# A mamba and mixture-of-experts layer on one core: the same steps in another order on every engine

## The reference

```python
h = layernorm(x) * (1 + ca) + sa
zxbcdt = h @ W_in                       # 256 -> 1288: z 512, xBC 768, dt 8
xBC = silu(causal_conv4(xBC) + conv_b)
dt = softplus(dt + dt_bias)             # cumulative sums of dt*A give the decays
y = ssd(x, dt, A, B, C) + x * D         # 8 heads of 64, 128 states
y = rmsnorm(y * silu(z)) * norm_w
x = x + ga * (y @ W_out)
h = layernorm(x) * (1 + cb) + sb
w = softmax(h @ gate_w + gate_b); w = normalise(where(w >= 0.1, w, 0))
x = x + gb * sum_e w[e] * (h @ expert_w[e] + expert_b[e])      # 8 experts, 256 x 256
```

## Time and profile before

| what | us |
|---|---|
| median of three runs | 2529.53 (2528.25 to 2530.95) |
| the profiled execution, its own time | 2541.7 |
| its span, first to last instruction | 2539.9 |
| PE busy | 2344.5 (92%) |
| DVE busy | 1958.5 (77%) |
| ACT busy | 1716.6 (68%) |
| POOL busy | 1618.7 (64%) |

### The profile page before, as it was taken

One profiled execution on the slowest core, in us unless ns is written; L12 is line 12 of the kernel. 1 busy time (PEld: TensorE's weight loads), 2 busy tenths in 40 slices (PEclk: granted clock), 3 DMA queues, 4 the chain that ended last, 5 costly groups with the idle time before them and its releaser, 6 DMA issues. The chain is left out here.

```text
span 2539.9 us, 48735 instructions
## 1 busy us (share of the span) xinstructions
PE 2344.5 (92%) x14936; PEld 1941.9 (76%) x14936; DVE 1958.5 (77%) x4070; ACT 1716.6 (68%) x4364; POOL 1618.7 (64%) x1812
## 2 busy tenths in 40 slices
PE   2689999999999999999999999999999999999998
PEld 2567787787778787778777777878777878777776
DVE  4378887887787887788788778788878878877863
ACT  1377776777777677776677777767777767777662
POOL 1145666766666676666676666667666667666676
PEclk6599999999999999999999999999999999999999
DMA  3000000000000000000000000000000000000000
GB/s 106 13 16 18 24 11 25 26 24 24 24 20 14 26 26 24 22 24 12 24 26 24 22 26 20 14 26 26 24 22 24 11 25 26 24 22 18 16 13 21
DMA packets 62927, 59.12 MB, mean 23 GB/s; under 512 B 10096, under 2 KB 62160, under 8 KB 62672
## 3 DMA queue, kind: packets, MB, share of 16 engines
q1 hardware_dynamic: 62672, 56.01, 7.2%
HBM read 39.22 MB, written 16.78 MB: 22 GB/s over the span
## 5 line engine op out<-in xcount | busy, mean ns | idle before, releaser
L858 DVE SCALAR_TENSOR_TENSOR feat<-pa,cw,feat 128x512 f32<-128x512 f32 x576 | 429.4, 745 | 73.4 <-ACT feat L547 65.2
L1163 PE MATMUL pe<-e_hi,h_hi 128*128 128x512 f32 x1024 | 448.6, 438 | 4.4 <-ACT eacc L682 2.3
L1163 PE MATMUL pe<-e_lo,h_hi 128*128 128x512 f32 x1024 | 413.1, 403 | 0.0
L1163 PE MATMUL pe<-e_hi,h_lo 128*128 128x512 f32 x1024 | 412.1, 402 | 0.0
L547 ACT ACTIVATE feat<-pa,cb,cw 128x512 f32<-128x512 f32 x192 | 149.3, 778 | 289.9 <-PE pa L1163 289.9
L1048 DVE SCALAR_TENSOR_TENSOR eacc<-pe,wg,eacc 128x256 f32<-128x256 f32 x512 | 245.3, 479 | 104.4 <-PE pe L1163 94.0
L620 ACT ACTIVATE lm<-lm,lndt 128x128 f32<-128x128 f32 x1024 | 325.1, 395 | 0.0
L609 ACT ACTIVATE lm<-pd,e3in 128x128 f32<-128x128 f32 x1024 | 278.8, 387 | 55.1 <-PE pd L1163 53.5
L401 POOL TENSOR_TENSOR rs<-ssq,neghalf 128x1 f32<-128x1 f32 x128 | 70.4, 550 | 356.7 <-ACT ysq L636 356.7
L1163 PE MATMUL pa<-h_hi,w_hi 128*128 128x260 f32 x768 | 244.5, 318 | 49.1 <-DVE feat L858 24.8
L692 ACT ACTIVATE ex<-pe,wg 128x256 f32<-128x256 f32 x512 | 212.9, 468 | 82.9 <-issue 43.8
(11 more groups left out here) (173 smaller groups left out, 6555.4 us busy)
## 6 DMA issues: line engine op xcount, KB each, us to landing
xin<-_attn_hidden_states_dram SPq DMA_DIRECT2D x32, 512.0 KB, 4.3
xres<-_attn_hidden_states_dram SPq DMA_DIRECT2D x128, 128.0 KB, 2.1
out_dram<-x SPq DMA_DIRECT2D x128, 128.0 KB, 2.2
feat<-in_L_wmod_dram SPq DMA_DIRECT2D x1, 1536.0 KB, 6.6
feat<-in_L_attn_W_in_dram SPq DMA_DIRECT2D x1, 1024.0 KB, 5.9
gz<-in_L_ffn_expert_w_dram SPq DMA_DIRECT2D x1, 1024.0 KB, 9.0
x<-in_L_ffn_expert_w_dram SPq DMA_DIRECT2D x1, 1024.0 KB, 11.3
mm<-in_L_attn_W_out_dram SPq DMA_DIRECT2D x1, 512.0 KB, 6.9
```

What stands on the lines that cost most here:

```text
L858: dve.scalar_tensor_tensor(out=acc, in0=pa[:, :, 1 + j:1 + j + HT], scalar=cw[:, f, j:j + 1], in1=acc, op0=ALU.mult, op1=ALU.add).then_inc ...
L1163: return pe.matmul(o, lhsT=l, rhs=r, start=start, stop=stop, skip_group_check=True)
```

## The change

Only the order in the five lists is new. Every step is issued as often as before, for the same tiles, with the same waits in it and on the same engine; no buffer changes. POOL's loop starts one pass earlier, so that `halo` can be written as `n + 4`. PE's list has the same 72 steps and DVE's the same 101; ACT's has 69, POOL's 55, SP's 9. The order differs in nearly every place. The piece of the diff around the cumulative sums, DVE first, then PE, then POOL:

```diff
             for n in range(-4, NTILE + 16, T):
...
                 do(dts_, dve, n - 4)
-                do(S_, dve, n - 6)
-                do(xD0, dve, n - 12)
-                do(xn2_, dve, n - 8)
+                do(xn2_, dve, n - 7)
+                do(x2_, dve, n - 6)
                 do(n_hi, dve, n)
                 do(cse_, dve, n - 4)
-                do(xn2_, dve, n - 7)
-                do(yTlo_, dve, n - 6)
-                do(gs_, dve, n - 5)
                 do(parts_, dve, n - 4)
+                do(M_, dve, n - 5)
+                do(st2_, dve, n - 6)
+                do(xD0, dve, n - 12)
+                do(es_, dve, n - 4)
+                do(lg_, dve, n - 8)
                 do(n_hi, dve, n + 2)
-                do(M_, dve, n - 5)
-                do(xD1, dve, n - 12)
-                do(y1_, dve, n - 5)
-                do(es_, dve, n - 4)
                 do(S_, dve, n - 5)
...
+                do(state_, pe, n - 5)
                 do(cs_, pe, n - 4)
-                do(xT_, pe, n - 5)
+                do(h2T_, pe, n - 8)
+                do(e3_, pe, n - 12)
                 do(hT_, pe, n + 2)
-                do(e2, pe, n - 12)
-                do(h2T_, pe, n - 8)
-                do(yoff_, pe, n - 5)
+                do(e0, pe, n - 12)
+                do(lgm_, pe, n - 8)
+                do(bias_, pe, n - 11)
                 do(csT_, pe, n - 4)
-                do(wout_, pe, n - 6)
-                do(ft0, pe, n)
-                do(bias_, pe, n - 11)
-                do(state_, pe, n - 5)
-                do(lgm_, pe, n - 8)
                 do(ydiag_, pe, n - 5)
                 do(D_, pe, n - 4)
+                do(xT_, pe, n - 4)
+                do(ft0, pe, n)
...
                 do(ve2_, pool, n - 8)
                 do(out_, pool, n - 14)
-                do(halo, pool, n)
-                do(y2_, pool, n - 6)
+                do(scd_, pool, n - 5)
+                do(xd_, pool, n - 5)
+                do(rs_, pool, n - 6)
+                do(rstd2_, pool, n - 8)
+                do(xs_, pool, n - 5)
                 do(exs_, pool, n - 13)
-                do(scd_, pool, n - 6)
-                do(rstd2_, pool, n - 8)
                 do(exb_, pool, n - 13)
                 do(n_lo, pool, n)
+                do(x2r_, pool, n - 6)
                 do(eall_, pool, n - 13)
-                do(h2lo_, pool, n - 10)
-                do(xs_, pool, n - 5)
                 do(og_, pool, n - 13)
+                do(exs_, pool, n - 12)
                 do(n_lo, pool, n + 2)
```

More of the change, by code:

```diff
@@ L448, in out_ @@
                 pool.tensor_tensor(x2[:, x.n % NX2], ex[:, x.j, 0], x2[:, x.n % NX2], ALU.add).then_inc(S["out"], 1)
-            for n in range(0, NTILE + 16, T):
+            for n in range(-4, NTILE + 16, T):
+                do(eall_, pool, n - 15)
+                do(exs_, pool, n - 14)
+                do(n_ve, pool, n)
+                do(exb_, pool, n - 14)
+                do(n_rstd, pool, n)
+                do(og_, pool, n - 15)
+                do(x2r_, pool, n - 8)
                 do(out_, pool, n - 15)
[L452 to L455, removed]
+                do(h2lo_, pool, n - 10)
+                do(xs_, pool, n - 6)
@@ L1077, in _ @@
+                do(xD1, dve, n - 15)
                 do(tA3, dve, n - 4)
-                do(ag2_, dve, n - 9)
-                do(xD0, dve, n - 14)
                 do(tB3, dve, n - 4)
                 do(tC3, dve, n - 4)
-                do(yTlo_, dve, n - 8)
-                do(y1_, dve, n - 7)
-                do(xn2_, dve, n - 10)
-                do(xn2_, dve, n - 9)
+                do(n_st, dve, n + 3)
+                do(x2_, dve, n - 8)
+                do(lg_, dve, n - 10)
+                do(M_, dve, n - 7)
@@ L1382, in _ @@
-                do(bias_, pe, n - 13)
-                do(h2T_, pe, n - 10)
-                do(wout_, pe, n - 8)
-                do(e1, pe, n - 13)
-                do(lgm_, pe, n - 10)
-                do(ft5, pe, n - 4)
-                do(e0, pe, n - 13)
+                do(wout_, pe, n - 8)
+                do(h2T_, pe, n - 10)
+                do(e3_, pe, n - 14)
+                do(lgm_, pe, n - 10)
+                do(ft4, pe, n - 4)
+                do(e0, pe, n - 14)
+                do(state_, pe, n - 7)
@@ L1403, in _ @@
-                do(bias_, pe, n - 12)
-                do(yoff_, pe, n - 6)
-                do(D_, pe, n - 5)
-                do(z_, pe, n - 1)
-                do(e1, pe, n - 12)
-                do(ydiag_, pe, n - 6)
-                do(state_, pe, n - 6)
-                do(hT_, pe, n)
-                do(e0, pe, n - 12)
-                do(e3_, pe, n - 12)
+                do(bias_, pe, n - 13)
+                do(ft5, pe, n - 4)
+                do(xT_, pe, n - 6)
+                do(e2, pe, n - 14)
@@ new lines, in _ @@
+                do(G_, pe, n - 6)
+                do(yT_, pe, n - 7)
+                do(e1, pe, n - 13)
+                do(yoff_, pe, n - 6)
+                do(wout_, pe, n - 7)
+                do(e0, pe, n - 13)
+                do(z_, pe, n - 4)
+                do(D_, pe, n - 5)
+                do(state_, pe, n - 6)
+                do(z_, pe, n - 3)
+                do(ydiag_, pe, n - 6)
+                do(z_, pe, n - 2)
+                do(xT_, pe, n - 5)
+                do(e3_, pe, n - 13)
@@ L1413, in _ @@
                 do(yT_, pe, n - 6)
                 do(G_, pe, n - 5)
+                do(z_, pe, n - 1)
+                do(gt_, pe, n - 12)
+                do(e2, pe, n - 13)
+                do(wgT_, pe, n - 12)
+                do(yoff_, pe, n - 5)
+                do(hT_, pe, n)
+                do(bias_, pe, n - 12)
+                do(wout_, pe, n - 6)
+                do(e1, pe, n - 12)
+                do(state_, pe, n - 5)
                 do(cs_, pe, n - 4)
-                do(xT_, pe, n - 5)
+                do(h2T_, pe, n - 8)
```

274 lines of the change are left out of this document (129 added, 145 removed).

## The result

The changed kernel takes 2378.77 us (2377.07 to 2385.10), the kernel before, timed beside it, 2530.24 us (2528.25 to 2532.53): a ratio of 0.9406, 95% interval 0.9386 to 0.9425. The profiled execution of the changed kernel took 2377.07 us, its span is 2375.3 us, against 2539.9 us before, so the two traces differ by 164.6 us.

What follows compares the result with a forecast made beforehand. PE's own work was taken as the bound: 70.9 + 0.2 + 1.15 + 0.5 + 0.15 = 72.9 us a group against 75.06, 58 us over 27 groups plus 1.9 at the end, giving 2470 us, range 2440 to 2532.

Steps and rivals of the forecast that it cites:

- PE's own work sets the pace and cannot shrink: Steady groups: PE's busy 70.9 us a group stays, as no instruction is removed; only idle and low-clock time can be won.
- wait between `csT_` and `ft0`: PE waits about 1.15 us a group there in small pieces, instead of 1.6 + 0.65 = 2.25.
- small waits shown (taps, `yT_`): PE waits 0.5 us a group for convolution taps and for `yT_` behind ACT's decays; bounds 0 and 1.3.
- low clock: Steady groups: PE's clock drops cost 0.15 us a group instead of 0.64; bounds 0 and 0.64.
- share of `gt_`: The extra `gt_` step in some groups adds 0.2 us to the average group.
- From `cs_` to `ft0`: Path through DVE and POOL takes 9.0 us beside 7.86 us of PE's own work.
- The low clock follows these two gaps: PE's clock falls after its standstills of 1.6 us before `csT_` and 0.65 us before `ft0`.
- Nothing: Start, to 383 us: bound by conv taps and loads that keep their durations, so no gain.
- At the end: Six expert steps instead of three cover PE's idle time ahead of the expert weights' transpose, so 1.9 us go.
- POOL's queue comes late: POOL's `ve2_` waits for DVE's later `ag2_`, delaying fifteen steps behind it; slower, about 2546 us at 5.3 us late; chance 0.13.
- Turns eat most of it: DVE and POOL block each other, PE waits 2.6 us at `ft0`; 2496 to 2524 us; chance 0.20.
- All of it: `parts_` meets less of POOL, the path fits into 7.86 us; 71.3 us a group, 2430 us; chance 0.11.

Runs made afterwards that it cites:

- light_after: Changed kernel with convolution taps, decays, `M_` and POOL's sums of y and experts' results cut to 8 columns, own order kept; 2348.64 us.
- light_before: Kernel before with convolution taps, decays, `M_` and POOL's sums of y and experts' results cut to 8 columns, old order kept; 2366.87 us.
- turns_after: Changed kernel with POOL's `h2lo_` moved back between the two `n_lo`, so one more POOL operation is ready beside `parts_`; 2417.17 us, ratio 0.9522 to the kernel before.
- cover_less: Changed kernel with one expert step, `e3_`, moved on PE from behind `cs_` and `h2T_` to ahead of `cs_`; 2435.97 us, ratio 0.9603 to the kernel before.
- lgm_before: Kernel before with `lgm_` moved on PE to directly behind `csT_`; 2521.59 us, ratio 0.9942.
- parts_first: Kernel before with `parts_` moved on DVE to right behind `cse_`, ahead of `xn2_`, `yTlo_` and `gs_`; 2588.64 us, ratio 1.0191.
- pe_cover: Kernel before with `ft0` moved two steps back on PE, behind `bias_` and `lgm_`; 2530.78 us, ratio 0.9984.
- light_lgm: light_before with `lgm_` moved on PE to directly behind `csT_`; 2353.66 us.
- light_g: light_lgm with one `G_` moved on PE from ahead of `gt_` and `xT_` to behind `xT_`; 2358.88 us.

## Why the prediction was right and wrong

The direction and the place were right. PE's idle time was the larger part of what an order could win, the largest piece of it stood at `csT_` and `ft0`, and turns between DVE and POOL made `parts_` late. The size was not. The 2.84 us a group between forecast and result come from two steps: the floor under PE's time (1.3), and the waits that I expected to stay (1.15 and 0.5).

**The step that failed: "PE's own work sets the pace and cannot shrink".** I took the busy 70.89 us of a group as a floor and could then win at most 3.3 us of idle time. The floor is no higher than 69.2 us, by `light_after`. For the old list `light_before` shows 1.0 us of waits inside the busy time, and by the estimate above, with the two waits for the state taken off, it is 1.5 us and 69.4 are left. A group lost 74.24 - 69.6 = 4.6 us undisturbed, more than all its idle time. With this floor even a forecast without any wait would have had 70.9 + 0.2 = 71.1 us a group, 107 us less, or about 2420, where 2379 was measured. The size of the other step, the waits that were to stay, is taken apart under the table.

**The sum against the measurement**, for a group, in us:

| term | forecast | measured |
|---|---|---|
| PE's own work, small hidden waits included | 70.9 | 69.6 |
| wait between `csT_` and `ft0` | 1.15 | 0 |
| small waits shown (taps, `yT_`) | 0.5 | 0 |
| low clock | 0.15 | 0.2 |
| share of `gt_` | 0.2 | 0.23 |
| sum | 72.9 | 70.06 |

The row on the clock is the mean of 70.06 less 69.6 and less the `gt_` share (six groups with about 1.03 us more). The 2.84 us between the sums make 77 us over 27 groups.

**From `cs_` to `ft0`.** The path was forecast at 9.0 us, 8.9 without the handover, and measured at 8.10 (775.81, the start of `cs_`, to 783.91). `parts_` has 1.95 instead of 2.98: I had counted how many operations POOL has ready there and not how long they are. `es_` has 0.5 instead of 0.9. `M_` has 1.68 instead of 1.13, which fits a wait for POOL's `og_` (778.49 to 779.27). The cover is 8.44 and not 7.86. So a wait of 1.15 became 0.24 to spare. `turns_after` shows that the 2.98 had not been a bad number for the case it was made for: with one more POOL operation in reach the four take 2.92. The path was treated as a sum of fixed prices; `cover_less`, with 0.9 us for the same four, shows that it is not.

**Small waits.** Forecast at 0.5, with 0 as a bound. The profile shows none. Some 0.4 us a group may be hidden, the difference of 69.6 to the light form's 69.2.

**The clock.** The amount was right (0.15 against 0.2 us), the reason only half, so there was luck in it. "The low clock follows these two gaps" may hold for part of the cases (`lgm_before`); `light_before` shows falls with no gap, right behind a row of narrow matmuls, and so do the four low stretches that stay in a kernel whose PE stands still for 0.5 us. In `cover_less` and `turns_after` low stretches in 13 and 11 groups came on top of the waits.

**Start and end.** "Nothing" was wrong for the start: 21.2 us. In its first two groups PE waited 10.4 us for convolution taps before, 2.9 after; the pace of the third and fourth group is already that of the steady part (73.58 to 69.59, 75.02 to 70.63). So 8.4 us of the 21.2 are these two groups, and 12.6 the first two. The light kernels, with nearly equal starts (340.8 and 341.9), speak for waits for other engines; which of them was not tested by itself. The granted clock of the first two groups also rose, from 0.83 and 0.90 to 0.94 both, and how much of the 12.6 us that is was not separated. At the end I forecast 1.9 and got 8.4, of which PE's busy time has 7.2 (113.4 to 106.2 us); this was not taken apart further. Steady part 77, start 21.2 and end 6.5 make 105 us, the difference between a forecast saving of 60 and the span's 164.6.

**The rivals.** "POOL's queue comes late" did not happen; POOL stands still for 1.3 and 0.8 us in the stretch shown, and nobody waits for it. Its sum had fifteen steps behind `ve2_` where the list has fourteen, which makes its threshold 0.9 us later. "Turns eat most of it" did not either: the turns are there, but short ones. "All of it" was nearest, with 2430, and it was held up by the same false floor: its best group was 71.3.

## What to carry to other kernels

Don't take an engine's busy time as what it needs: sum its steps by their shortest start-to-start times, or run the kernel with the other engines' work cut to a few columns and read the group's length. Take the start of a step to the start of the next, since its idle time shows only part of a wait. When one wait is moved, read what the next two steps on the waiting engine wait for, since in a list this full they are next (`parts_first`, `pe_cover`). Where tiny VectorE operations stand on the critical chain, give GpSimd none but its shortest work beside them. When a step is moved to test one wait, look where the new wait stands before its size is believed (`cover_less`). Count ScalarE's table loads whenever its list is reordered. If the clock falls behind narrow matmuls in one row, try one of them elsewhere (`light_lgm`).

## What the runs showed of the hardware

- A short wait appears only in part as idle time of PE: one of 0.74 us (2.22 less 1.48) was shown as 0.58, one of 0.5 as 0.25, one of 0.41 (1.91 less 1.50) as 0.24.
- The granted clock fell to 0.52 with PE 100% busy, behind matmuls of 8 and of 64 columns and on 24 rows in a row; with the 8-column step elsewhere (`light_lgm`, `light_g`) it did not fall in 27 groups.
- One low stretch costs a group 1.5 to 1.7 us in the changed kernel (71.1 to 71.3 against 69.6), 1.5 in the light old one (71.6 against 70.1), and 0 to 1.1 in `lgm_before`, where PE waits in every group.
- DVE operations on 32 columns take 0.19 us alone and 0.4 to 1.2 us beside a busy POOL; one more POOL operation of 1.27 us in reach of four of them costs 0.95 us, and with POOL mostly past (`cover_less`) the four take 0.9 us in all.
- A load of ScalarE's function table takes 1.28 us; the new order has 64 of them at line 520 where the old has 128.
